# QKV projection and attention put into one block of a conv-scan-attention kernel

## The reference

```
t = t + attn(ln(t));  t = t + ffn(ln(t))
qkv = x @ W_qkv; q, k, v of 4 heads x 32 channels
q, k = q / norm(q), k / norm(k)     # the norm is over the 4096 TOKENS, per channel
attn = softmax(10 * q k^T);  out = (attn v) @ W_out + b_out
```

## Time and profile before

| | us |
|---|---|
| median of 3 runs | 5550.67 |
| the profiled execution, its own time | 5559.32 |
| its span | 5557.6 |
| VectorE busy | 4864.6 (88%) |
| TensorE busy | 4773.5 (86%) |
| ScalarE busy | 4017.6 (72%) |

### The profile page before, as it was taken

How to read it: one execution, slowest core, us unless ns; L and a number is a source line. 1 busy time by engine, 2 the same in 40 slices (tenths; PEclk the granted TensorE clock), 3 DMA queues, 4 the chain that set the end, 5 groups by cost and what they waited for, 6 DMA issues and landing times. The chain is left out here.

```text
span 5557.6 us, 100602 instructions
## 1 busy us (share of the span) xinstructions
PE 4773.5 (86%) x34168; PEld 1985.8 (36%) x34168; DVE 4864.6 (88%) x6244; ACT 4017.6 (72%) x5832; POOL 1610.2 (29%) x790
## 2 busy tenths in 40 slices
PE   5888879998778887999877887899987788789998
PEld 2333333334333333333433333333343333333334
DVE  6799779998789977999868997799986899689998
ACT  4787569994477757999447784799935778479993
POOL 1388700000048860000004885000000588500000
PEclk9899989999899998999988999899998899999998
DMA  1000030000000003000000000300000000030000
GB/s 41 0 1 0 16 66 10 10 6 24 24 0 1 0 16 66 10 10 6 24 24 0 1 0 16 66 10 10 6 23 24 1 1 0 16 66 10 10 6 31
DMA packets 42112, 89.63 MB, mean 16 GB/s; under 512 B 11595, under 2 KB 27798, under 8 KB 38550
## 3 DMA queue, kind: packets, MB, share of 16 engines
q1 hardware_dynamic: 41622, 83.21, 5.6%
HBM read 28.65 MB, written 8.39 MB: 7 GB/s over the span
## 5 line engine op out<-in xcount | busy, mean ns | idle before, releaser
L1576 ACT ACTIVATE arena<-ps 128x1024 f32<-128x1024 f32 x2048 | 1912.6, 1034 | 190.5 <-PE ps L1539 168.8
L1605 DVE TENSOR_TENSOR arena<-arena 128x1024 f32<-128x1024 f32 x1664 | 1899.6, 1216 | 17.8 <-ACT arena L1576 17.6
L1188 DVE TENSOR_TENSOR_SCAN arena<-ps,hlast,arena 128x512 f32<-128x512 f32 x1024 | 1251.5, 1265 | 28.3 <-ACT hlast L1070 13.9
L1133 POOL TENSOR_TENSOR arena<-arena 128x1024 f32<-128x1024 f32 x512 | 1201.6, 2357 | 240.2 <-ACT arena L1049 173.7
L1539 PE MATMUL ps<-arena 128*32 128x512 f16 x16384 | 1091.0, 382 | 111.2 <-issue 81.0
L1522 PE MATMUL ps<-arena 128*32 128x512 f32 x8192 | 1068.4, 600 | 7.3 <-ACT arena L1576 3.6
L955 PE MATMUL ps<-arena,ident 128*128 128x512 f32 x2048 | 964.8, 595 | 0.0
L1067 ACT ACTIVATE ps<-arena,amat 128x512 f32<-128x512 f32 x1024 | 704.5, 688 | 354.4 <-DVE arena L1188 345.4
L1539 PEld LDWEIGHTS ps<-arena 128*32 128x32 f16 x16384 | 464.6, 97 | 965.9 <-issue 667.8
L1911 POOL MEMSET arena<- 128x1024 f32 x4 | 3.8, 952 | 2452.5 <-POOLq L103 2452.5
L1164 DVE TENSOR_TENSOR arena<-arena,ps 128x1024 f32<-128x1024 f32 x416 | 497.4, 1196 | 80.9 <-PE ps L1024 80.9
(11 more groups left out here) (283 smaller groups left out, 4518.4 us busy)
## 6 DMA issues: line engine op xcount, KB each, us to landing
arena<-x SPq DMA_DIRECT2D x36, 512.0 KB, 5.2
arena<-arena SPq DMA_DIRECT2D x64, 256.0 KB, 6.0
arena<-arena SPq DMA_DIRECT2D x64, 224.0 KB, 5.8
arena<-arena SPq DMA_DIRECT2D x28, 512.0 KB, 3.7
arena<-pe SPq DMA_DIRECT2D x256, 32.0 KB, 1.8
out<-arena SPq DMA_DIRECT2D x8, 1024.0 KB, 3.9
expw<-L_ffn_expert_w SPq DMA_DIRECT2D x1, 512.0 KB
wqkv<-L_attn_W_qkv SPq DMA_DIRECT2D x1, 192.0 KB
```

The lines of the kernel that those rows point to most:

```text
L1133: pool.tensor_tensor(halves(hb[s % RING]), halves(hb[s % RING]), cs[s % 4].unsqueeze(1).broadcast_to([128, HD, CH]), ALU.mult).then_inc(hc ...
L1188: dve.tensor_tensor_scan(halves(hb[s % RING])[:, h, :], da(s, h), halves(injected)[:, h, :], k.hlast[:, s, h, :], ALU.mult, ALU.add).then_ ...
L1576: act.activation(probs[p % 8], k.bank(2 * group[p], 2 * CH), ACT.Exp, scale=SCALE / SPLIT ** 2).then_inc(exp_s, 1)
L1605: dve.tensor_tensor(acc[p % 2], acc[p % 2], probs[p % 8], ALU.add).then_inc(acc_s, 1)
```

## The change

`qkv` goes; its instructions become the class `Projected`, and the block `attention` runs them ahead of the branch on each engine, with no barrier between. Inside:

- VectorE copies the 8 key chunks and query chunks 3 to 7 from PSUM to the arena; ScalarE copies query chunks 0 to 2. ScalarE squares from the arena copy and not from PSUM. TensorE may use a bank again once its copy is made.
- The maxima of the squares are gone. The guard takes the largest of the 8 chunk sums of squares in their place, sums the products over the 32 channels of each head, and compares the largest of the 4 heads with (60/10)^2/32.
- The keys are split and stacked in three parts (columns 0 to 1023, 1024 to 2047, 2048 to 4095), each with its 16 DMAs and its semaphore. ScalarE makes the high half of the third part. The scores of chunk 0 wait for each part where it is first needed.
- The first 512 stacked queries have a place of their own; the DMAs for the others now cover all 4096 columns (16 of 256 KB, before 224 KB).
- The table for Exp is loaded after the squares, ahead of the values' Copies.
- The branch is turned round: the unguarded code comes first, the guarded one behind it.
- The split halves of the queries lie where `tnt` was, so their writes wait until TensorE has read it (the `vmm` waits).

```diff
-QF_AT, KF_AT, KH_AT, KL_AT, QH_AT, QL_AT = 0, 4096, 8192, 10240, 40960, 24576
+QF_AT, KF_AT, KH_AT, KL_AT, QH_AT, QL_AT = 0, 4096, 24576, 26624, 28672, 30720
+STAGE_AT, SUM0_AT, Q0_AT = 24576, 40960, 43008
+KEY_PARTS = ((0, 1024), (1024, 2048), (2048, 4096))
...
+    def tensor(self, pe):
...
+                if m == self.Q_:
+                    self.wait_kept(pe, self.K_, c)
+                pe.matmul(k.bank(c), k.wqkv[:, at:at + C], self.tnt[:, c * CH:(c + 1) * CH], start=True, stop=True).then_inc(self.mm, 1)
+        for g in range(NG):
+            if g == 4:
+                pe.wait_ge(self.u_s, 1)
+                self.wait_kept(pe, self.Q_, NCH - 1)
+                pe.matmul(k.bank(7, 128)[0:1, :], self.u, k.ident[:, :], start=True, stop=True).then_inc(self.umm, 1)
+            self.wait_kept(pe, self.Q_, g)
+            if g == 7:
+                pe.wait_ge(self.flag_s, 1)
...
+        pe.wait_ge(self.q0_split, 1)
+        for h in range(HEADS):
+            pe.wait_ge(self.vev, h + 1)
...
+        pe.wait_ge(self.vev, NG)
+
+    def scalar(self, act):
...
+        for m in (self.K_, self.Q_):
+            for c in range(NCH):
+                act.wait_ge(self.mm, m * NCH + c + 1)
+                if m == self.Q_ and c < self.by_scalar:
+                    act.activation(self.full[m][:, c * CH:(c + 1) * CH], k.bank(c), ACT.Copy).then_inc(self.kept_a, 1)
+                self.wait_kept(act, m, c)
+                act.activation(self.square[m][:, c * CH:(c + 1) * CH], self.full[m][:, c * CH:(c + 1) * CH], ACT.Square,
+                               accum_out=self.part[:, 0, m, c:c + 1]).then_inc(self.sq_s, 1)
+            root(m)
+        k.ready_table(act, ACT.Exp, 1)
+        for g in range(NT // 4):
+            act.wait_ge(self.vmm, g + 1)
+            act.activation(self.v[:, g * CH:(g + 1) * CH], k.bank(g), ACT.Copy).then_inc(self.vev, 1)
+            if g == 1:
+                a, b = KEY_PARTS[2]
...
+                act.activation(self.hi[self.K_][:, a:b], self.full[self.K_][:, a:b], ACT.Identity, scale=self.sc[:, 0:1])\
+                    .then_inc(self.k2_high, 1)
+        for h in range(HEADS):
+            act.wait_ge(self.q0_mm, h + 1)
+            act.activation(first_queries(k)[:, h, :], k.bank(h), ACT.Copy).then_inc(self.q0_s, 1)
+        act.wait_ge(self.flag_s, 1)
+
+    def vector(self, dve):
...
+        for c in range(NCH):
+            keep(self.K_, c)
+        scale(self.K_)
+        bound(self.K_)
+        times_split(self.K_)
+        self.wait_kept(dve, self.K_, NCH - 1)
+        split(self.K_, *KEY_PARTS[0], self.kh_s)
+        for c in range(self.by_scalar, NCH):
+            keep(self.Q_, c)
+        scale(self.Q_)
+        bound(self.Q_)
+        dve.tensor_tensor(self.u, mx[:, 0:1], mx[:, 1:2], ALU.mult).then_inc(self.u_s, 1)
+        times_split(self.Q_)
+        self.wait_kept(dve, self.Q_, 0)
+        dve.wait_ge(self.vmm, 5)
+        split(self.Q_, 0, CH, self.q0_split)
+        split(self.K_, *KEY_PARTS[1], self.kh_s)
...
+        dve.wait_ge(self.umm, 1)
+        step(dve.reduce_sum(per_head, k.bank(7, 128)[0:1, :].rearrange("p (h d) -> p h d", h=HEADS), axis=AX.X))
+        step(dve.reduce_max(most, per_head, axis=AX.X))
+        dve.tensor_scalar(k.flag[0:1, 0:1], most, (SAFE / SCALE) ** 2 / DH, None, ALU.is_gt).then_inc(self.flag_s, 1)
+        a, b = KEY_PARTS[2]
+        dve.wait_ge(self.k2_high, 1)
+        dve.scalar_tensor_tensor(self.lo[self.K_][:, a:b], self.full[self.K_][:, a:b], sc[:, self.K_:self.K_ + 1],
+                                 self.hi[self.K_][:, a:b], ALU.mult, ALU.subtract).then_inc(self.kh_s, 1)
...
+        dve.wait_ge(self.vmm, NT // 4)
+        split(self.Q_, CH, L, self.q_split)
+        dve.wait_ge(self.flag_s, 1)
+
+    def sync(self, sp):
+        k = self.k
+        for n, (a, b) in enumerate(KEY_PARTS):
+            sp.wait_ge(self.kh_s, n + 1)
+            stack_heads(k, sp, KS_AT, KH_AT, KL_AT, (0, 2), a, b, self.key_s[n])
+        sp.wait_ge(self.q0_split, 1)
+        sp.wait_ge(self.q_split, 1)
+        stack_heads(k, sp, QS_AT, QH_AT, QL_AT, (0, 1), 0, L, k.sem("q_rest"))
...
@@ attend, tensor: body
+                    if first(c) and p < 2:
+                        pe.wait_ge(projected.q0_s, 2 * a + 2)
+                    if first(c) and a == 0 and j * 128 in key_parts:
+                        pe.wait_ge(projected.key_s[key_parts.index(j * 128)], 4 * HEADS * 16)
...
@@ attention, on each of the three engines
-            with pe.If(need == 1):
-                guarded[0](pe)
-            with pe.Else():
-                bounded[0](pe)
+            projected.tensor(pe)
...
+            with pe.If(need == 0):
+                bounded[0](pe)
+            with pe.Else():
+                guarded[0](pe)
```

More of the change, by code:

```diff
@@ L1356, in stack_heads @@
             sp.dma_start(stack[32 * g:32 * g + 32, h, a:b], src[32 * h:32 * h + 32, a:b]).then_inc(done, 16)
[L1359 to L1468, removed]
@@ L1471, in staged_queries, with attend @@
 def staged_queries(k):
-    return [k.at(QL_AT + i * 2 * CH, 2 * CH).bitcast(F16).rearrange("p (h n) -> p h n", h=HEADS) for i in range(2)]
-def attend(k):
+    return [k.at(STAGE_AT + i * 2 * CH, 2 * CH).bitcast(F16).rearrange("p (h n) -> p h n", h=HEADS) for i in range(2)]
+def attend(k, projected):
     qs, ks = (k.at(a, 2 * L).bitcast(F16).rearrange("p (h n) -> p h n", h=HEADS) for a in (QS_AT, KS_AT))
@@ L1483, in attend @@
     probs = [k.at(8192 + i * 2 * CH, 2 * CH) for i in range(8)]
-    sums = [[k.at(at + i * 2 * CH, 2 * CH) for i in range(2)] for at in (SUM_AT, QH_AT)]
+    sums = [[k.at(at + i * 2 * CH, 2 * CH) for i in range(2)] for at in (SUM0_AT, SUM_AT)]
     rl = k.at(RL_AT, CH)
@@ L1529, in finish @@
             ones_by(sums[q], False, True).then_inc(l_mm, 1)
+        key_parts = [a for a, b in KEY_PARTS]
         def body(c, q, queries):
@@ L1556, in staged @@
             body(c, i, q_now[i])
-        body(0, 0, qs[:, :, 0:CH])
+        body(0, 0, first_queries(k))
         with pe.Fori(0, NCH // 2 - 1) as cc:
@@ L1580, in scalar @@
         act.sem_inc(exp_s, 3)
-        k.ready_table(act, ACT.Exp, 1)
         body(0)
@@ L1618, in attend, with attend_guarded @@
     return tensor, scalar, vector
-def attend_guarded(k):
+def attend_guarded(k, projected):
     qs, ks = (k.at(a, 2 * L).bitcast(F16).rearrange("p (h n) -> p h n", h=HEADS) for a in (QS_AT, KS_AT))
@@ L1645, in tensor @@
         pe.wait_ge(k.sem("q_rest"), 4 * HEADS * 16)
+        pe.wait_ge(projected.q0_s, HEADS)
+        for s in projected.key_s:
+            pe.wait_ge(s, 4 * HEADS * 16)
         with pe.Fori(0, NCH) as c:
@@ L1728, in attention @@
 def attention(k):
-    guarded, bounded = attend_guarded(k), attend(k)
+    projected = Projected(k)
+    guarded, bounded = attend_guarded(k, projected), attend(k, projected)
     with k.nc.Block() as block:
@@ L1734, in _ @@
         def _(sp):
-            stack_heads(k, sp, QS_AT, QH_AT, QL_AT, (0, 1), CH, L, k.sem("q_rest"))
-            sp.wait_ge(k.sem("q_rest"), 4 * HEADS * 16)
+            projected.sync(sp)
             staged_s = [k.sem("q_even_staged"), k.sem("q_odd_staged")]
@@ L1741, in _ @@
                     sp.wait_ge(k.sem("scores_mm"), (c - 1) * 2 * (L // 128))
+                    sp.wait_ge(staged_s[c % 2], 16 * ((c - 1) // 2))
                 sp.dma_start(staged_queries(k)[c % 2], qs[:, :, cols_of(c)]).then_inc(staged_s[c % 2], 16)
@@ L1756, in _ @@
         def _(act):
+            projected.scalar(act)
             need = act.value_load(k.flag[0:1, 0:1], min_val=0, max_val=1)
-            with act.If(need == 1):
+            with act.If(need == 0):
+                bounded[1](act)
+            with act.Else():
                 guarded[1](act)
-            with act.Else():
-                bounded[1](act)
             act.drain()
@@ L1765, in _ @@
         def _(dve):
+            projected.vector(dve)
             need = dve.value_load(k.flag[0:1, 0:1], min_val=0, max_val=1)
-            with dve.If(need == 1):
+            with dve.If(need == 0):
+                bounded[2](dve)
+            with dve.Else():
                 guarded[2](dve)
-            with dve.Else():
-                bounded[2](dve)
             dve.drain()
```

79 lines of the change are left out of this document (78 added, 1 removed).

## The result

The changed kernel takes 5505.08 us (median of 4 runs, 5502.05 to 5510.85), the one before 5551.1; ratio 0.9913, 95% interval 0.9897 to 0.9929. It is faster by 46 us where 86 were forecast, and lies outside the range of 5440 to 5497. The profiled execution took 5510.85 us against 5559.32.

The account below looks back on a forecast made before the run. VectorE was taken to bound attention, whose end moves with its start on chunk 0. Per image -20.8 - 1.1 + 0.3 = -21.6 us, four images -86: median 5465, own range 5456 to 5474, whole range 5440 to 5497.

Parts of the forecast that it names:

- VectorE's first copy: Start of attention's chunk 0 on VectorE: at 751.3 against 772.09, 20.8 us earlier per image.
- idle time in chunk 0: VectorE's 2.2 us of idle time in attention's chunk 0: 0 to 2.2 us goes, 1.1 taken.
- end jump: TensorE's jump over the guarded code at attention's end, beside VectorE's last work: costs 0 to 0.4 us, 0.3 taken.
- attention's end moves with the time at which VectorE can start chunk 0: Whole of attention: an earlier VectorE start carries to its end, provided that scores arrive in time; 20.8 us.
- chunk 1: Attention's second query chunk: VectorE's first copy of it at 812 to 815, before at 835.85.
- Theory A: Experiments' theory, after the forecast: attention's start came as forecast, and the missing part is in jumps of the code.
- the key and query chains: Projection stage: first key part split by 731.4, first 512 queries by 739.4, the other queries by 750.3.
- first score: TensorE's first score matmul in attention: at 747, or 750 to 752 with a slow branch; before 769.94.
- no part of the keys came late: Stacking DMAs: none late; the rival, keys late with the branch still slow, had 17.1 us an image, 5482, chance 0.10.
- TensorE's branch: Branch into attention: 0.1 us where it took 4.56, as the unguarded code now follows directly.
- a TensorE that comes in at its low clock: Rival, attention gives back part of its start: chunk 0 grows 2 to 5 us, 5475 to 5483, chance 0.14.

Follow-up runs that it names:

- e6: The kernel before the change with the query-chunk loops of TensorE, ScalarE and VectorE written out: 5511.3 us.
- e5: The changed kernel with the query-chunk loops of TensorE, ScalarE and VectorE written out: 5439.6 us.
- e1: The changed kernel with only TensorE's loop over query chunks 1 to 6 written out: 5454.8 us.
- e2: The changed kernel with 32 empty semaphore increments on TensorE's queue just ahead of its loop: 5493.4 us.
- e9: The changed kernel, loops kept, with 32 empty semaphore increments at the end of TensorE's unsort block, where it waits anyway: 5477.4 us.
- e7: e5 with SyncE starting the keys' stacking DMAs only when all three key parts have been split: 5469.1 us.
- e8: e5 with the sixteen maxima per image put back on VectorE ahead of each scale, results unused: 5469.3 us.
- e10: e5 with the old order of the branches, guarded code first, on all three engines: 5429.7 us.
- e4: The changed kernel, loops kept, with only the order of the two branches undone on all three engines: 5485.4 us.

## Why the prediction was wrong

Per image, forecast and measured (means of the table, after against before):

| term | forecast | measured |
|---|---|---|
| VectorE's first copy | -20.8 | -20.6 |
| idle time in chunk 0 | -1.1 | -1.4 |
| loop, chunks 2 to 5 | 0 | +7.3 |
| end jump | +0.3 | +2.2 |
| image | -21.6 | -12.6 |

(The lines above add up to -12.5; chunks 6 and 7 are 0.6 longer, the other stages 0.7 shorter.)

**The step that failed** is in the first paragraph: "attention's end moves with the time at which VectorE can start chunk 0". It took everything behind the start as unchanged. The trace of the kernel before spoke against that: 69.1 and 68.1 us for chunks 2 and 4 beside 65.3 for chunk 1 were there to be asked about, and I read only the first three copies of the earlier trace rows. The kernel before pays for its jumps back (9.1 us per image in chunks 2 to 5, by e6), the changed one pays 16.4 (by e5), and what is paid depends on where the loop's top lies. e1, e2 and e9 show that: 7.3 us per image, 29 of the missing 40. Theory A came from a rule that I had weighed for the branch into attention and for the jump at its end, but not for the loop. "Runtime: NRT & Kernel Launch" of the Trainium skill, "Instruction fetch mechanics", has it that prefetch is sequential and that a taken branch out of the window forces a fetch. The trace agrees on two engines: TensorE's jump back takes 3.4 to 3.9 us when taken and 0.083 when not, with 2.59 us of idle time behind it that nothing ends, and VectorE idles 3.84 us behind its own. ScalarE's jump back (0.05 us, no gap) shows no such stall. That the time goes into fetching code is the page's account of it; the runs show that it stands at the jumps, goes with them and changes with their place. What exactly a second stall needs was not tried beyond one shift of 32.

**The end jump** was given to the wrong engine. TensorE's does lie beside VectorE's last two instructions, as worked out: it takes 3.3 to 4.0 us in the four images, in the first from 1282.3 to 1285.6. In this line the four branches at the start (75 ns the least) are mixed with the four jumps at the end:

```profile
L1826 PEldq COMPARE_BRANCH  x8: 75/1690/4005, 745.9 to 5387.6; - x8
```

But VectorE jumps too. I priced its jump at 0.07 us from the earlier trace rows, where it lay ahead of 7 us of waiting for the first exp, so that any fetch behind it cost nothing and left no trace. A branch's own duration is not its price on VectorE: its jump back takes 0.06 us in its own row (line 1612 of the kernel before) and is followed by 3.84 us of idle time.

**Right by their sizes:** the key and query chains, first score, first copy, chunk 1; the issue of 64 KB DMAs (forecast 0.5 us, measured 0.59, and 0.63 from one start to the next), and that no part of the keys came late: they had landed at 743.9, 755.3 and 767.6 (forecast 743, 753 and 763; wanted at 747, 763 and 779). VectorE's copies from PSUM take 0.69 us, from start to start 0.60 when nothing else holds them. After:

```profile
L1358 SPq DMA_DIRECT2D arena<-arena x256: 507/591/2026, 732.3 to 4883.9; - x128
...
DMA to landing us min/median/max: 2.0/2.3/8.8
```

e7 and e8 show two of the parts at work, 9 us per image each. TensorE's branch was priced right at the start (0.1 for 4.56 us), yet e10 shows that it was worth only 3 us there: with the branch back, VectorE's first copy comes 1.0 us later, as it stood 4 us behind the first score, and chunk 0 is 1.7 us longer.

**Partly:** "a TensorE that comes in at its low clock" did occur, in images 3 and 4, where first score and first copy are 2.8 and 1.4 us later than in images 1 and 2. The clock falls there behind TensorE's wait of 2.31 us for the flag; the same wait stands in image 1, where the selection's eight matmuls take 1.89 us and not 3.05. The stretches of image 4, with the queries' selection in the second:

```profile
4844.00:4848.00 4.00, 1.69 (x17) 1.53 (x15) 3.82 (x8) 4.00 (x6) 0.00 (x0) 1.00 0.45 108
4848.00:4852.00 4.00, 4.00 (x15) 2.39 (x16) 4.00 (x2) 1.94 (x4) 0.00 (x0) 0.57 0.44 105
```

**Open:** what decides, behind a wait of TensorE, whether the clock falls. It is worth some 3 us per image between kernels whose blocks outside attention are the same (e5, e10), so a difference of 10 us between two runs here says little of the edit. In e4, too, the end jump's 2.2 us are gone and other blocks took them back. Nor was it tried whether the DMA that stages queries, which runs at the jump back (0.55 DMA share from 941 to 944), makes the stall longer; it doesn't make the difference between one stall and two, as it is there in both kernels (0.56 before).

## What to carry to other kernels

Where a kernel has loops or branches with long bodies, look at the first iterations side by side before taking any of it as constant: chunks that differ by 4 us under equal work are a cost that an edit elsewhere can double or halve. Compare versions with the loops written out, or at two places in the code: the same change measured 46 us in one place and 72 us without loops. And look for the price of a jump in the idle time behind it, on every engine that takes it, since the one that waits for something else hides it. Last, split a small difference by stage before it is given to the edit: of the 10 us between e5 and e10, what was edited had lost.

## What the hardware showed that was not expected

- 32 instructions without effect, put where TensorE waits, made the kernel 28 us faster (5505.1 to 5477.4), 26 of it by the loop (6.5 us per image); 32 of them on its busy queue cost 3.4 us in one chunk, 0.11 us each.
- A stall of 2.6 us on TensorE was followed by half clock for some 6 us (0.50 from 944 to 950), where eight matmuls took 2.24 us that take 1.04 before it, so that a jump costs more than its own time.
- ScalarE's squares from SBUF take 0.61 to 0.63 us for 512 columns, no longer than the 0.59 to 0.85 that they took from PSUM.
